# Two graph networks on one core: setup's head in two parts, dense blocks over 43 steps, float32 edge sums

## The reference

```python
# first network: three layers, per layer
msg = relu(x[src]) + 1e-7
out = softmax_aggregate(msg, dst) + x     # per destination and feature
h = out @ W1 + b1                         # 128 -> 256
h = relu(batch_norm(h over all nodes))
x = relu(h @ W2 + b2)
# second network: three layers, per layer
h = relu(x @ nw.T); e = relu(ea @ ew.T)
e2 = concat([h[src] + h[dst], e])
agg = segment_sum(e, dst)                 # the edge sums
x = bn(relu(concat([agg, h]) @ fnw.T + fnb))
ea = relu(e2 @ few.T + feb)
# around each network: x = x + network(relu(layernorm(x)))
```

## Time and profile before

| | us |
|---|---|
| median of 3 runs | 3490.31 |
| lowest and highest run | 3484.79, 3492.27 |
| the profiled execution's own time | 3487.84 |
| its span in the trace | 3486.0 |
| PE busy | 3110.1 (89%) |
| POOL busy | 2383.1 (68%) |
| DVE busy | 2049.3 (59%) |
| ACT busy | 1873.9 (54%) |

### The profile page before, as it was taken

One profiled execution on the slowest core, in us unless ns is written; L12 is line 12 of the kernel. 1 busy time (PEld: TensorE's weight loads), 2 busy tenths in 40 slices (PEclk: granted clock), 3 DMA queues, 4 the chain that ended last, 5 costly groups with the idle time before them and its releaser, 6 DMA issues.

```text
span 3486.0 us, 67856 instructions
## 1 busy us (share of the span) xinstructions
PE 3110.1 (89%) x19129; PEld 2564.2 (74%) x19129; DVE 2049.3 (59%) x4862; ACT 1873.9 (54%) x3489; POOL 2383.1 (68%) x2488
## 2 busy tenths in 40 slices
PE   2799997858889699999789999886999999999998
PEld 0466664657778577788777888775888888888887
DVE  7665553234545656455556455584676766777675
ACT  0432222735556487666577666584555555555554
POOL 3777777777777366777355777426777777777773
PEclk7799998979999899999899999998999999999998
DMA  9587555368888377888467888566555665655652
GB/s 347 179 282 226 183 181 163 95 187 268 266 266 269 100 254 239 276 279 270 128 220 235 278 279 270 181 185 196 156 163 165 166 166 164 164 164 165 166 165 79
DMA packets 419112, 713.35 MB, mean 205 GB/s; under 512 B 75585, under 2 KB 259067, under 8 KB 416098
## 3 DMA queue, kind: packets, MB, share of 16 engines
q0 software_dynamic: 130688, 321.08, 30.8%
q1 hardware_dynamic: 270119, 323.69, 30.6%
q10 hardware_dynamic: 18107, 66.24, 5.0%
HBM read 561.35 MB, written 149.39 MB: 204 GB/s over the span
## 4 chain that ended last, share of the span: by engine, by line
PE 49%; POOL 25%; issue 10%; DVE 5%; ACT 3%; DMA 3%; ACTq 2%; SPq 1%; DVEq 1%; POOLq 0%
POOL pair_rings L674 16%; PE ps L1614 5%; PE ps L2260 5%; PE ps L2299 5%; PE ps L2281 5%; PE ps L2293 5%; POOL adjacency L689 5%; PE ps L2310 5%; POOL end_rows L674 3%; PE ps L736 3%; PE ps L724 3%; PE ps L742 3%; PE ps L2262 3%; PE ps L728 2%; ACTq L962 2%
## 5 line engine op out<-in xcount | busy, mean ns | idle before, releaser
L2250 POOL DMA_INDIRECT ring<-h_table,idx_ring x832 | 806.4, 969 | 259.7 <-issue 229.4
L674 POOL DMA_INDIRECT pair_rings<-split_table,src_idx x728 | 729.6, 1002 | 255.5 <-issue 222.8
L1614 PE MATMUL ps<-casts,two_parts 128*128 128x500 f32 (+1 forms) x3464 | 785.8, 382 | 64.6 <-DVE two_parts L1704 51.6
L1614 PEld LDWEIGHTS ps<-casts,two_parts 128*128 128x128 f32 x3464 | 633.2, 194 | 181.5 <-DVE two_parts L1704 53.7
L689 POOL DMA_INDIRECT adjacency<-edge_counts,places_of_counts x508 | 499.4, 983 | 207.5 <-issue 155.9
L1510 ACT ACTIVATE casts<-spare 128x1000 fp32r<-128x1000 fp8e4 (+1 forms) x471 | 458.9, 974 | 9.9 <-DMA spare<-adjacency 6.1
L1704 DVE TENSOR_TENSOR two_parts<-work,two_parts 128x512 fp32r<-128x512 f32 (+1 forms) x276 | 187.6, 680 | 465.1 <-ACT two_parts L1500 465.1
L2347 ACT ACTIVATE work<-acc,vecs 128x512 f32<-128x512 f32 x208 | 150.2, 722 | 384.7 <-DVE acc L2404 324.5
L1637 PE MATMUL ps<-pair_rings,hot_r 128*128 128x256 f32 x1680 | 245.2, 296 | 90.6 <-DMA pair_rings<-split_table,src_idx 79.9
L1500 ACT ACTIVATE two_parts<-work 128x512 fp32r<-128x512 f32 (+1 forms) x276 | 170.5, 618 | 281.2 <-PE ps L1614 272.0
L1637 PEld LDWEIGHTS ps<-pair_rings,hot_r 128*128 128x128 f32 x1680 | 216.5, 195 | 103.1 <-issue 46.7
(11 more groups left out here) (329 smaller groups left out, 6241.2 us busy)
## 6 DMA issues: line engine op xcount, KB each, us to landing
spare<-adjacency SPq DMA_DIRECT2D x216, 250.0 KB
acc<-e_few SPq DMA_DIRECT2D x208, 256.0 KB
work<-msg_table SPq DMA_DIRECT2D x144, 256.0 KB, 4.8
work<-in_edge_attr SPq DMA_DIRECT2D x104, 256.0 KB
e_few<-spare SPq DMA_DIRECT2D x52, 512.0 KB
spare<-rel_rows SPq DMA_DIRECT2D x208, 84.0 KB
spare<-adjacency SPq DMA_DIRECT2D x72, 187.5 KB
e_few<-work SPq DMA_DIRECT2D x26, 512.0 KB
```

The source lines that it names most:

```text
L674: e.indirect_dma_start(out=to, out_offset=None, in_=table, in_offset=bass.IndirectOffsetOnAxis(ap=src_idx[:, 2 * i + h, j:j + 1], axis=0)) ...
L1614: ins = e.matmul(bank, parts_of(d)[:, b % 2, q, kind * D:(kind + 1) * D], cast_counts[n % CASTS][:, at:at + width], start=opens, stop=(b = ...
L2250: e.indirect_dma_start(out=rows[:, s, j, :], out_offset=None, in_=h_table, in_offset=bass.IndirectOffsetOnAxis(ap=idx_ring[:, s, j:j + 1], ...
```

## The change

It has four parts.

1. *Setup's head.* Addresses and counts are worked out in two parts, segment 0 alone and then segments 1 to 3 (39 compares and 78 matmuls each). The first 127 scatters wait for the first part and for region 0's three fills alone; the others for the second part, and the 128th for the rest of the fills.
2. *The dense start.* SP loads the first rows, then the first counts, then the second rows. In layer 0 its wait for the early scatters moves ahead of these counts and rows. ACT makes the first high part ahead of the first cast.
3. *The dense blocks over 43 steps.* `STEPS` = `PAIRS` + 1: the last step of blocks stands behind the sums of the last pair. The last blocks of the regions move from steps 2, 16, 30, 41 to 2, 17, 31, 42 in layer 0 and from 7, 20, 32, 41 to 7, 20, 33, 42 in layers 1 and 2; the last step has 4 blocks in layer 0 and 5 in the others. The tail's order becomes 2000 | 5500, 5750 | 2250 | 6000, and all but the first stand behind the loop.
4. *The edge sums.* One plain float32 matmul a block of 128 edges instead of two fp32r ones; the copy on ACT, the subtraction on DVE and their buffers go, and the sums, the one-hot matrix and what follows come one step earlier.

```diff
+STEPS = PAIRS + 1
-        return (before - lead) * PAIRS // (BLOCKS * sum(columns) - lead)
+        return (before - lead) * STEPS // (BLOCKS * sum(columns) - lead)
-    return FIRST_STEPS + (before - first) * (PAIRS - FIRST_STEPS) // (BLOCKS * sum(columns) - first)
+    return FIRST_STEPS + (before - first) * (STEPS - FIRST_STEPS) // (BLOCKS * sum(columns) - first)
...
                 if i == 0:
-                    e.wait_ge(S("zero_fill"), 16 * FILLS * 2)
+                    e.wait_ge(S("zero_fill"), 16 * FILLS)
                 if i == WIDE:
-                    e.wait_ge(S("zero_fill_rest"), 16 * (FILLS * (len(REGIONS) - 2) + 1))
+                    e.wait_ge(S("zero_fill_rest"), 16 * (FILLS * (len(REGIONS) - 1) + 1))
...
+        NEAR_PARTS = (slice(0, 1), slice(1, SEGMENTS))
         def repeats_pe(e, S):
-            for k in range(1, NEAR + 1):
-                e.wait_ge(S("hit"), k)
-                e.matmul(ps[0][:, 0:COLS], ident_b, same[k % 4][:, :, k:k + WIDE], start=(k == 1), stop=(k == NEAR))
-                e.matmul(ps[1][:, 0:COLS], ident_b, same[k % 4][:, :, 0:WIDE], start=(k == 1), stop=(k == NEAR)).then_inc(S("counted"), 1)
+            made = 0
+            for g in NEAR_PARTS:
+                to = slice(g.start * WIDE, g.stop * WIDE)
+                for k in range(1, NEAR + 1):
+                    hits = same[made % 4]
+                    made += 1
+                    e.wait_ge(S("hit"), made)
+                    e.matmul(ps[0][:, to], ident_b, hits[:, g, k:k + WIDE], start=(k == 1), stop=(k == NEAR))
+                    e.matmul(ps[1][:, to], ident_b, hits[:, g, 0:WIDE], start=(k == 1), stop=(k == NEAR)).then_inc(S("counted"), 1)
...
+            for of_segments in NEAR_PARTS:
+                g = of_segments
...
+                for k in range(1, NEAR + 1):
+                    n = WIDE + k
+                    if made >= 4:
+                        e.wait_ge(S("counted"), made - 3)
+                    e.tensor_tensor(same[made % 4][:, g, 0:n], key[:, g, NEAR - k:NEAR + WIDE], key[:, g, NEAR:NEAR + n], ALU.is_equal).then_inc(S("hit"), 1)
+                    made += 1
...
+                then(e.tensor_tensor(to_places[:, g, :], to_places[:, g, :], low_i[:, g, :], ALU.bitwise_or))
+                e.sem_inc(S("addresses"), 1)
...
                 e.wait_ge(S("addresses"), 1)
-                scatters(e, S, 0, EARLY)
+                scatters(e, S, 0, WIDE)
+                e.wait_ge(S("addresses"), 2)
+                scatters(e, S, WIDE, EARLY)
...
-                for j in range(2):
-                    load_dense_rows(j)
+                load_dense_rows(0)
                 if ready:
                     scattered(e, S, EARLY)
-                for d in range(3):
+                load_counts(0)
+                load_dense_rows(1)
+                for d in range(1, 3):
                     load_counts(d)
...
+                    if d == 0:
+                        dense_high(d)
                     cast_block(first_block(d))
-                    dense_high(d)
+                    if d > 0:
+                        dense_high(d)
...
                     if i == PAIRS:
                         W1_of_tail(e, S, TAIL[0])
-                        W1_of_tail(e, S, TAIL[1])
...
-                    if i == PAIRS + len(REGIONS[-1][1]) - 1:
-                        W1_of_tail(e, S, TAIL[2])
-                W1_of_tail(e, S, TAIL[3])
+                for part_of_tail in TAIL[1:]:
+                    W1_of_tail(e, S, part_of_tail)
...
+            edge_hots = flat_hot[:, 0:RING * J * W].rearrange("p (s j w) -> p s j w", s=RING, j=J)
...
-                    if (i - 6).inside(NG):
-                        k = i - 6
+                    if (i - 5).inside(NG):
+                        k = i - 5
                         s = k.off % RING
-                        wait(e, S("low"), k)
+                        wait(e, S("e2"), k)
...
                         for j in range(J):
-                            for q in range(2):
-                                ins = e.matmul(ps[7][:, 0:W], parts[k.off % 4][q][:, j, :], edge_hots[:, s, j, :],
-                                               start=(j == q == 0), stop=(j == J - 1 and q == 1))
+                            ins = e.matmul(ps[7][:, 0:W], ring[:, s, j, ROW:ROW + D], edge_hots[:, s, j, :],
+                                           start=(j == 0), stop=(j == J - 1))
...
-                        e.activation(parts[k.off % 4][0], ring[:, k.off % RING, :, ROW:ROW + D], ACT.Copy).then_inc(S("high"), 1)
...
-                            ins = e.tensor_tensor(parts[k.off % 4][1][:, j, :], ring[:, k.off % RING, j, ROW:ROW + D],
-                                                  parts[k.off % 4][0][:, j, :].bitcast(F32), ALU.subtract)
```

More of the change, by code:

```diff
@@ L165 @@
         [(node, least, sparse) for _, node, least, sparse in LATE if not sparse and least == FIRST_OF_LAST],
[L166 to L167 removed]
+        [(node, least, sparse) for _, node, least, sparse in LATE if sparse and least == PAIRS],
+        [(node, least, sparse) for _, node, least, sparse in LATE if not sparse and least > FIRST_OF_LAST]]
 NJOBS = len(JOBS_OF[0]) + len(LATE)
@@ L762, in addresses_dve @@
             later, earlier = in_segments(ps[0][:, 0:COLS]), in_segments(ps[1][:, 0:COLS])
+            counts_f8, to_places = in_segments(count_8.bitcast(F8)), in_segments(spread_i)
             e.wait_ge(S("near"), 32)
             then(e.tensor_copy(ident_b, ident[:, :]))
[L765 to L792, removed]
@@ L801, in addresses_dve @@
-            then(e.tensor_tensor(low_f, low_f, spread_f, ALU.add))
-            then(e.tensor_copy(in_segments(spread_i), high_f))
-            then(e.tensor_copy(low_i, low_f))
-            then(e.tensor_tensor(in_segments(spread_i), in_segments(spread_i), low_i, ALU.bitwise_or))
-            e.sem_inc(S("addresses"), 1)
+            made = 0
+            for of_segments in NEAR_PARTS:
+                g = of_segments
+                then(e.tensor_copy(src_f[:, g, :], in_segments(near_src)[:, g, :]))
+                then(e.tensor_copy(dst_f[:, g, :], in_segments(near_dst)[:, g, :]))
+                for k in range(g.start, g.stop):
+                    then(e.tensor_scalar(key[:, k, :], dst_f[:, k, :], dst_f[:, k, 0:1], float(SPAN), ALU.subtract, ALU.mult))
+                if g.stop == SEGMENTS:
+                    then(e.tensor_reduce(small[:, 18:19], key[:, g, :].rearrange("p s c -> p (s c)"), AX, ALU.max))
+                else:
+                    then(e.tensor_reduce(small[:, 20:21], key[:, g, :].rearrange("p s c -> p (s c)"), AX, ALU.max))
+                then(e.tensor_tensor(key[:, g, :], key[:, g, :], src_f[:, g, :], ALU.add))
+                for k in range(1, NEAR + 1):
[4 more added lines that the diff above has]
+                    made += 1
+                s, d = src_f[:, g, own], dst_f[:, g, own]
+                low, high, other, kept = low_f[:, g, :], high_f[:, g, :], spread_f[:, g, :], kept_edge[:, g, :]
+                then(e.tensor_scalar(low, d, float(CUT + REGIONS[1][0]), None, ALU.is_ge))
+                for at, widths in REGIONS[2:]:
+                    then(e.tensor_scalar(high, d, float(CUT + at), None, ALU.is_ge))
+                    then(e.tensor_tensor(low, low, high, ALU.add))
+                then(e.tensor_scalar(high, low, float(SPAN), None, ALU.mult))
+                then(e.tensor_scalar(low, low, -float(REGIONS[1][0]), -float(CUT), ALU.mult, ALU.add))
+                then(e.tensor_tensor(low, low, d, ALU.add))
+                then(e.tensor_tensor(high, high, s, ALU.add))
+                then(e.tensor_scalar(kept, d, float(CUT), None, ALU.is_lt))
+                then(e.tensor_scalar(other, d, float(N), None, ALU.is_ge))
+                then(e.tensor_tensor(kept, kept, other, ALU.max))
+                e.wait_ge(S("counted"), made)
+                then(e.tensor_scalar(counts_f8[:, g, :], later[:, g, :], 1.0, None, ALU.add, saturate=False))
+                then(e.tensor_scalar(other, earlier[:, g, :], 0.0, None, ALU.is_gt))
+                then(e.tensor_tensor(kept, kept, other, ALU.max))
+                then(e.tensor_tensor(spread[:, g, :], spread[:, g, :], high, ALU.subtract))
+                then(e.tensor_tensor(spread[:, g, :], spread[:, g, :], kept, ALU.mult))
+                then(e.tensor_tensor(high, high, spread[:, g, :], ALU.add))
+                then(e.tensor_scalar(high, high, float(PITCH), None, ALU.mult))
+                then(e.tensor_scalar(other, low, iota_t[:, 0:1], -1.0, ALU.subtract, ALU.mult))
+                then(e.tensor_tensor(other, other, kept, ALU.mult))
+                then(e.tensor_tensor(low, low, other, ALU.add))
+                then(e.tensor_copy(to_places[:, g, :], high))
+                then(e.tensor_copy(low_i[:, g, :], low))
+                then(e.tensor_tensor(to_places[:, g, :], to_places[:, g, :], low_i[:, g, :], ALU.bitwise_or))
+                e.sem_inc(S("addresses"), 1)
```

(1 more changed line is left out.)

62 lines of the change are left out of this document (18 added, 44 removed).

## The result

The changed kernel took 3454.34 us (median of 4 runs) against 3489.19 (4 runs): ratio 0.9905, 95% interval 0.9889 to 0.9921. The forecast was 3459. The profiled execution took 3454.95 itself, its span is 3453.1 us, 32.9 shorter than before. Each experiment's lines are numbered in its own file.

What follows compares the result with a forecast made beforehand. POOL's queue was taken to bound up to layer 0's gathers and later gathers, PE and POOL the edge layers. Terms -22.5 - 4.4 + 3.4 - 5.8 + 0 - 1.6 = -30.9 gave 3456.9, as median 3459; range 3447 to 3478.

Steps and rivals of the forecast that it cites:

- the 27.9 worked out for them: Setup's head: region 0's zero fills could hold the first scatter until 27.9 us, before the 31.1 forecast for its start.
- its lower price for the compares: Setup's head: 0.33 us per DVE compare, from an operation on 166 elements; 0.40 was taken, 0.70 the upper price.
- The cover of DVE's double work: Setup: DVE's 6 to 7 us of extra work stays hidden in its 16.2 us idle wait for ACT.
- the middle taken: Dense start of layers 1 and 2: a gain of 2.2 us in each, -4.4 in all.
- the upper bound of 2.6: Dense start: gain per layer if the counts land earlier by the whole 2.29 us wait.
- the dense end T: Layer's end: last gather issue + 4.74 + 2.0 for sums + last step's blocks; statistics end at T + 15.5 us.
- PE is there in time in both: Layer ends 0 and 1: the step taken from before the last sums frees PE 5.5 to 6.9 us ahead.
- the forecast -2.9 a layer: Ends of layers 1 and 2: statistics end 2.9 us sooner in each, -5.8 together; layer 2 taken as layer 1.
- rival C: Layer ends: PE at half rate after idling, 2.4 us more in each of three layers, 3466 us; chance 0.12.
- rival B: Edge sums: dearer fp32 records, +132 us to 3591, deciding from 0.130 a record; chance 0.07 with the +22 case, 0.04 slower.
- Steady: 0: Edge layers: eight PE records stay at 0.89 us, so no change in the steady phase, with -6 to +5.
- Rival D: Edge layers: less ACT and DVE work lets POOL run at its bare pitch, 3449 us, needing quicker PE; chance 0.06.

Runs made afterwards that it cites:

- `steps_only`: The kernel before with only the dense blocks over 43 steps and the new tail order: 3490.47 against 3490.54 us, ratio 0.9999.
- the late loads: Changed kernel with dense blocks on 42 steps again and SP's loads behind the addresses' two held until region 0's fills land: 3423.87 us, again 3423.12.

## Why the prediction was right, and where it was not

**Part 1** was right in size (-22.3 for -22.5), by two errors that cancel. The compares cost 0.23, not 0.40, so the addresses were ready at 23.7 and not at 29.9; the fills then held the scatter to 28.75 (the last of them landed at 27.85, as the 27.9 worked out for them). Of the gain at the start, 25.0, the first 32 scatters lost 5.2 again, since DVE's second part lengthens POOL's issues: a cost that the prediction did not have. At scatter 128 19.3 were left, and before the first gather 3 us came back: layer 0's first gather stands 22.3 earlier, with the same 3.77 us ahead of it. (By the prediction's own sum its lower price for the compares, 0.33, puts the first scatter at 28.4, just behind the fills' 27.9, so that the fills bind there does not come out of it; at the measured 0.23 they do.) The cover of DVE's double work held, as forecast.

**Part 2** was right in mechanism, 0.4 to 0.5 a layer larger than the middle taken: -2.7 and -2.6, at the upper bound of 2.6.

**Part 3** was the step that failed, by its size in layers 1 and 2. Behind the dense end T the chain is as forecast: 16.0, 15.4 and 15.7 us in the three layers for 15.5. T itself was not: it was worked out from the landing of the last rows, "PE is there in time in both". In layer 1 PE came out of the step before at 1671.7, when all rows had just landed, so all sixteen sums stood ahead of the blocks, and T is 1.2 later than 4.74 + 2.0 + 6.9 behind the last issue; in layer 2 it is 2.2 later, and in layer 0 1.5 sooner. Layer 2 was taken as layer 1's, but its end before was 1.2 us shorter (30.9 for 32.1). That the forecast -2.9 a layer is not there shows in both kernels with part 3: from a layer's first block to the end of its statistics, layers 1 and 2 changed by -2.0 and +1.8 in the changed kernel, by -0.5 and +0.1 in `steps_only`. The idle time that would have cost the clock (rival C) did not come. What the prediction did not see at all is that part 3 is two changes of opposite sign, 8 to 11 us a layer each: it priced the new order only together with the step that delays it.

**Part 4** was right on PE's records: eight a group, no dearer, far from rival B's 0.130. Its size was off, -7.4 for -1.6, and so was the reason for "Steady: 0". The prediction took PE's records to set the step, and read a slack of 0.012 between POOL's pitch and a bare one. That slack is the first gather's own wait (6.5 us) spread over 832, and a handover of 0.305 for 0.30. In both traces every later gather starts within 0.32 us of the end of the one before it, so POOL sets the step of this phase, before and after, and what counts is how long its issue takes: 969 ns before, 962 after, and 832 times the difference is 6 us. From the first gather to group 200's the phase is 5.9 us shorter (a step of 5.064 for 5.081 us from group 48 on); it starts 1.3 later, the way from group 200 to PE's last sum gives 1.8, and the output behind it 1.0.

The traces also say which issues became shorter. All that take more than 0.97 us lie beside DVE's one-hot compare (L2384; L2391 in the changed kernel). Where that compare begins 0.3 us or more into an issue, 61 to 91 of some 170 are long in each of the five traces with fp32r sums, every one with a subtraction (L2431) beside it too, and none in the seven traces with float32 sums. So the subtractions had very likely lengthened them, as the compares do in setup; ACT's copy went together with them, and no run takes away one alone. Rival D named POOL's pitch at -10. The gain came from there, but by a shorter issue: there was no wait of POOL's to save, and PE did not have to be quicker.

The rule that spoke against part 4, the Trainium skill's on fast weight load ("TensorE: Matmul & The Clock Gate", section "Weight-path perf modes — Fast Weight Load (FWL) and DoubleRow"), did not bear here: with plain float32 weights eight records take 0.82 by their starts, the fp32r ones 0.89.

## What to carry to other kernels

Take a change of several parts apart before pricing it: here the order of the tail was worth 23 us alone by the times and 25 by the traces, the step that came with it gave that back, and the version without it (3427 and 3430 in two sets of runs, 3424 and 3423 with the late loads) beats both kernels. At a layer's end ask which instruction at the head of an in-order queue waits for another engine, and what stands behind it that could run now. When an early start is the gain, list every gate in front of it with its own time, since the next one takes over.

## What the runs showed of the hardware that was not expected

- POOL's indirect DMA issue can last longer beside a DVE operation of two tensors in SBUF. In the changed kernel's setup 12 issues beside a compare alone took 1.29 us on average (0.97 to 1.46), those beside the statistics of x (one tensor) 0.96, while the DMA engines were full in both cases; without the compares the pitch of 32 scatters fell from 1.45 to 1.27. Beside an addition that takes its second tensor from PSUM (L2404 in the edge layers before, 186 issues) an issue stays at 0.95. Not every issue beside two tensors in SBUF is longer: it depends on when in the issue the operation starts, as the edge layers show. The Trainium skill ("SBUF — State Buffer", section "Who interferes with whom") says that a DVE instruction with two inputs in SBUF contends with a GpSimd instruction that reads SBUF; these rows agree, if an issue counts as one that reads SBUF (its places and counts lie there).
- A plain float32 matmul of 42 columns stands as two records. Of a group's eight, the first two start 0.037 us apart and the others 0.106 to 0.112 (0.100 on average), where the fp32r ones follow by 0.112 throughout. The first of the eight starts 0.89 behind the first of L2312's eight, where the first fp32r one started 0.81 behind L2299's (3458.59 to 3459.40). Both groups of eight together take 0.89 + 0.82 = 1.71 against 0.81 + 0.89 = 1.70: the same.
